# Attention of one layer on one core: the values product two tiles behind the scores, projections in the spare halves of the score banks, three queues written in a new order, and the causal bias matmul moved from first to third place in its group

## The reference

```
q_latent, kv_latent = xn @ wq_down, xn @ wkv_down            # 192 and 64 wide
q = concat(q_latent @ wq_nope, rope(q_latent @ wq_rope))     # per head 128 + 64
k = concat(kv_latent @ wk_nope, rope(kv_latent @ wk_rope))
scores = where(causal, q k^T / sqrt(192), min);  probs = softmax(scores)
out = (probs @ (kv_latent @ wv_up)).reshape(b, t, 16 * 192) @ wo
x = x + out + mixture_of_experts(xn)                          # top 8 of 32 experts
```

## Time and profile before

| | us |
|---|---|
| median of 3 runs (lowest, highest) | 1311.97 (1310.3, 1316.01) |
| the profiled execution's own time | 1314.4 |
| its span, first to last instruction | 1312.6 |
| PE busy in the span | 1161.8 (89%) |
| DVE, ACT, POOL busy | 720.3 (55%), 646.2 (49%), 493.9 (38%) |
| attention, from its first score matmul to the first matmul of the experts | 69.3 to 901.7 |

### The profile page before, as it was taken

One profiled execution on the slowest core, in us unless ns is written; L12 is line 12 of the kernel. 1 busy time (PEld: TensorE's weight loads), 2 busy tenths in 40 slices (PEclk: granted clock), 3 DMA queues, 4 the chain that ended last, 5 costly groups with the idle time before them and its releaser, 6 DMA issues. The chain is left out here.

```text
span 1312.6 us, 23292 instructions
## 1 busy us (share of the span) xinstructions
PE 1161.8 (89%) x7616; PEld 936.2 (71%) x7616; DVE 720.3 (55%) x1298; ACT 646.2 (49%) x1287; POOL 493.9 (38%) x386
## 2 busy tenths in 40 slices
PE   6678889888888898898888988998999999999997
PEld 3456667667677676676776766776788887888886
DVE  6556756556555556565555565554444445444444
ACT  3545556555555565555555555664433333333332
POOL 1263534543444445335444453421333332333332
PEclk9989999999999999999999999998999999999999
DMA  5001001000000000100000000103633333533332
GB/s 194 33 0 32 1 1 32 1 0 26 5 0 2 28 0 0 31 0 0 31 0 0 15 0 1 57 25 97 198 112 115 112 114 107 143 114 111 113 112 88
DMA packets 26304, 67.35 MB, mean 51 GB/s; under 512 B 3029, under 2 KB 9557, under 8 KB 26265
## 3 DMA queue, kind: packets, MB, share of 16 engines
q1 hardware_dynamic: 26120, 66.78, 16.6%
q10 hardware_dynamic: 144, 0.07, 0.0%
HBM read 62.36 MB, written 4.47 MB: 51 GB/s over the span
## 5 line engine op out<-in xcount | busy, mean ns | idle before, releaser
L714 ACT ACTIVATE prob<-ps_s,nm 128x128 f32<-128x128 f32 (+7 forms) x256 | 189.5, 740 | 203.3 <-DVE nm L866 200.9
L1305 POOL TENSOR_TENSOR hl<-hf,hh 128x512 fp32r<-128x512 f32 x96 | 123.5, 1286 | 294.9 <-ACT hh L1242 294.9
L866 DVE TENSOR_REDUCE nm<-ps_s 128x1 f32<-128x128 f32 (+7 forms) x256 | 192.3, 751 | 70.5 <-PE ps_s L548 69.0
L571 PE MATMUL ps_o<-pt,kvn 128*64 128x128 f32 x2304 | 154.0, 277 | 64.5 <-DVE pt L875 49.5
L571 PEld LDWEIGHTS ps_o<-pt,kvn 128*64 128x64 f32 x2304 | 126.2, 136 | 100.9 <-ACT pt L724 51.2
L559 PE MATMUL ps_t<-ident,prob 128*128 128x128 f32 x1152 | 173.0, 276 | 9.4 <-DVE pt L875 6.7
L1017 POOL TENSOR_TENSOR xtf<-xtf,sinv 128x512 f32<-128x512 f32 x62 | 79.4, 1280 | 223.4 <-DVE xtf L835 221.2
L559 PEld LDWEIGHTS ps_t<-ident,prob 128*128 128x128 f32 x1152 | 138.7, 142 | 32.2 <-issue 10.9
L1032 POOL TENSOR_TENSOR qlo<-t,qhi 64x512 fp32r<-64x512 f32 x64 | 82.0, 1281 | 159.8 <-ACT qhi L751 147.2
L724 ACT ACTIVATE pt<-ps_t 128x128 f32<-128x128 f32 (+2 forms) x192 | 96.6, 503 | 88.1 <-PE ps_t L559 86.7
L875 DVE COPY pt<-ps_t 128x128 f32<-128x128 f32 (+2 forms) x192 | 101.6, 529 | 56.2 <-PE ps_t L559 55.3
(11 more groups left out here) (272 smaller groups left out, 2689.5 us busy)
## 6 DMA issues: line engine op xcount, KB each, us to landing
routing<-wT_scratch SPq DMA_DIRECT2D x34, 256.0 KB, 3.7
raw_a<-in_e SPq DMA_DIRECT2D x17, 384.0 KB, 3.1
cosv<-in_e SPq DMA_DIRECT2D x17, 384.0 KB, 3.1
sinv<-wT_scratch SPq DMA_DIRECT2D x17, 384.0 KB, 3.6
raw<-in_e SPq DMA_DIRECT2D x17, 384.0 KB, 3.0
routing<-wT_scratch SPq DMA_DIRECT2D x16, 384.0 KB, 3.3
raw_a<-in_a SPq DMA_DIRECT2D x8, 512.0 KB, 3.3
raw_b<-in_b SPq DMA_DIRECT2D x8, 480.0 KB, 3.9
```

Source lines behind the costliest of these rows:

```text
L571: mm = nc.tensor.matmul(ps_o[64 * e:64 * e + 64, at], kvn[:, b * 8 + j, :], pt[t % 2][:, e, j, :], start=j == 0, stop=j == t)
L714: nc.scalar.activation(prob[t % 2][e][:, 0:len(halves) * width].rearrange("p (h k) -> p h k", k=width), ps_s[e][:, 0:len(halves), 0:width] ...
L866: nc.vector.tensor_reduce(out=nm[:, e:e + 1], in_=ps_s[e][:, 0:len(halves), 0:halves[0][1]], axis=AXXY, op=ALU.max, negate=True).then_inc( ...
L1305: nc.gpsimd.tensor_tensor(hl[:, c, :], hf[:, c, :], hh[:, c, :].bitcast(F32), ALU.subtract).then_inc(h_lo, 1)
```

## The change

The values product of step `t` is now that of tile `t - 2` (`before_tile(..., lag=2)`), and it stands between the turns of head 0 and those of head 1 of tile `t - 1`, not at the end of the step. Six kinds of side work (`Lp`, `QR1`, `KR0`, `KR1`, and `W1`, `W3` of the last stage) no longer use `ps_x`: up to tile 3 the second bank of `ps_s[0]` or `ps_s[1]` lies idle, and they take it (`SPARE`, `bank_of`); the scores of tile 4 wait until it has been read. `STAGE` and the three queues of PE, ACT and DVE are written in a new order, and POOL takes the low part of the first `QR` after all four sums. The causal bias matmul stands between the second and the third fp32r pass. `split_a` reads PSUM first, so that the bank is free two operations earlier. No matmul, transpose, copy or transfer is added or taken away.

```
-STAGE = ["Lp", "QR0", "KR0", "QL0", "QR1", "L0", "Yp0", "KR1", "QL1", "Yp1", "B", "WA", "Y0", "Y1"]
+STAGE = ["QR0", "Lp", "KR0", "QL0", "QR1", "KR1", "Yp0", "Yp1", "L0", "B", "QL1", "WA", "Y0", "Y1"]
+SPARE = {"Lp": 0, "QR1": 0, "W3": 0, "KR0": 1, "KR1": 1, "W1": 1}
...
+    if spare is not None:
+        earlier = [x for x in order[:order.index((b, name))] if x[0] == b and SPARE.get(x[1]) == spare]
+        return (i, *earlier[-1]) if earlier else None
...
+            return ps_s[SPARE[name]][:, 1, :] if name in SPARE else ps_x
...
-        def before_tile(i, b, t):
+        def before_tile(i, b, t, lag=1):
             s = i * 2 + b
-            return (s, b, t - 1) if t else (s - 1, 1 - b, TILES - 1)
+            return (s, b, t - lag) if t >= lag else (s - 1, 1 - b, TILES + t - lag)
...
             if name == "WA":
-                return a_split, (0 if b is None else i + 1) * 4 + 4
+                return a_split, (0 if b is None else i + 1) * 4 + 2
...
+                if t == TPC and half == 1:
+                    held = ("KR1" if e else "QR1") if not is_last(i, b) else "W1" if e else "W3"
+                    pe.wait_ge(*consumed(i, b, held))
...
+                nc.tensor.matmul(out[:, 0:width], qhi[b][e][:, q], khi[b][e][:, kk], start=True, stop=False, skip_group_check=True)
+                nc.tensor.matmul(out[:, 0:width], qhi[b][e][:, q], klo[b][e][:, kk], start=False, stop=False, skip_group_check=True)
                 if diagonal:
-                    nc.tensor.matmul(out[:, width - P:width], mask16[:, :], ident16[:, :], start=True, stop=False, skip_group_check=True)
-                nc.tensor.matmul(out[:, 0:width], qhi[b][e][:, q], khi[b][e][:, kk], start=not diagonal, stop=False, skip_group_check=True)
-                nc.tensor.matmul(out[:, 0:width], qhi[b][e][:, q], klo[b][e][:, kk], start=False, stop=False, skip_group_check=True)
+                    nc.tensor.matmul(out[:, width - P:width], mask16[:, :], ident16[:, :], start=False, stop=False, skip_group_check=True)
                 mm = nc.tensor.matmul(out[:, 0:width], qlo[b][e][:, q], khi[b][e][:, kk], start=False, stop=True, skip_group_check=True)
...
+                        def products():
+                            if earlier or t > 1:
+                                values(*before_tile(i, b, t, 2))
...
                         elif t < TPC:
                             scores(i, b, t, 0, 0)
-                            turn(sp, tp, 0, 0)
-                            turn(sp, tp, 1, 0)
+                            turns(0)
+                            also("QL0" if t == 2 else "QR1")
+                            products()
+                            turns(1)
                             scores(i, b, t, 1, 0)
-                            values(sp, bp, tp)
-                            also(("KR0", "QL0", "QR1")[t - 1])
+                            if t == 3:
+                                also("KR1")
...
-                            also(("KR1", "Yp1", "WA")[t - TPC - 1])
-                            scores(i, b, t, 1, 0)
-                            turn(sp, tp, 1, 0)
-                            turn(sp, tp, 1, 1)
-                            scores(i, b, t, 1, 1)
+                            if t < TILES - 1:
+                                also(("L0", "QL1")[t - TPC - 1])
+                            products()
                             if t == TILES - 1:
                                 also("Y0")
-                            values(sp, bp, tp)
-                            also(("QL1", "B", "Y1")[t - TPC - 1])
+                            scores(i, b, t, 1, 0)
+                            turns(1)
+                            scores(i, b, t, 1, 1)
+                            also(("B", "WA", "Y1")[t - TPC - 1])
...
-                        rope_low(s + 1, 0, 1 - b, (rope_sum, s * 4 + 7))
-                        rope_low(s + 1, 1, 1 - b, (rope_sum, s * 4 + 7))
                         rope_sum_of(s + 1, 3)
+                        rope_low(s + 1, 0, 1 - b, (rope_sum, s * 4 + 8))
```

More of the change, by code:

```diff
@@ L660, in body @@
                             scores(i, b, t, 0, 0)
-                            turn(sp, tp, 0, 0)
                             scores(i, b, t, 0, 1)
-                            also("L0")
-                            turn(sp, tp, 1, 0)
+                            turns(0)
+                            also("Yp0")
+                            products()
+                            turns(1)
                             scores(i, b, t, 1, 0)
                             scores(i, b, t, 1, 1)
-                            values(sp, bp, tp)
@@ L668, in body @@
-                            also("Yp0")
+                            also("Yp1")
                         else:
@@ L688, in _ @@
             s, t = 2 * PAIRS - 1, TILES - 1
-            for e in range(2):
-                for g in range(2):
-                    turn(s, t, e, g)
+            for g in range(2):
+                turn(s, t, 0, g)
+            values(s, 1, t - 1)
+            for g in range(2):
+                turn(s, t, 1, g)
             pe.wait_ge(widened, s * 2 + 2)
@@ L912, in body @@
                         has = earlier or t > 0
+                        if more and t == 1:
+                            rope_products(i, b, "QR0", s + 1)
+                        if more and t == 2:
+                            rope_products(i, b, "KR0", s + 1)
+                        if more and t == 3:
+                            latent_low(i, b, 0, s + 1, 1 - b)
+                        if more and t == TPC:
+                            rope_products(i, b, "KR1", s + 1)
+                        if t == TPC + 1 and earlier:
+                            add_out(misc(i, b, "Yp1"), ps_x, s - 1, 1 - b, 1, 1)
@@ L913, in body @@
+                        if t == TPC + 2 and b == 0:
+                            split_b(i, b)
+                        if t == TPC + 3 and b == 0 and not is_last(i):
+                            split_a(i, b, i + 1)
+                        maximum(s, t, 0)
+                        if has and (t == 0 or t > TPC):
+                            take_turned(sp, tp, 0, 1)
                         if t == 0 and earlier:
                             invert(s - 1, 1)
+                        if more and t == 3:
+                            rope_products(i, b, "QR1", s + 1)
@@ L929, in body @@
-                        if more and t == TPC + 1:
-                            rope_products(i, b, "KR1", s + 1)
-                        if t == TPC + 2 and earlier:
-                            add_out(misc(i, b, "Yp1"), ps_x, s - 1, 1 - b, 1, 1)
-                        if t == TPC + 3 and b == 0 and not is_last(i):
-                            split_a(i, b, i + 1)
-                        if has and t > TPC:
-                            take_turned(sp, tp, 1, 1)
-                        maximum(s, t, 1)
@@ L938, in body @@
-                        if has and t == 0:
-                            take_turned(sp, tp, 1, 1)
-                        if t == 0 and earlier:
-                            normalise(s - 1, 1)
-                        if more and t in (0, 1, 3):
-                            rope_products(i, b, ("QR0", "KR0", None, "QR1")[t], s + 1)
-                        if more and t == 2:
-                            latent_low(i, b, 0, s + 1, 1 - b)
-                        if t == TPC:
-                            normalise(s, 0)
-                            if earlier:
-                                add_out(misc(i, b, "Yp0"), ps_x, s - 1, 1 - b, 1, 0)
@@ L952, in body @@
+                        if t == 1 and earlier:
+                            normalise(s - 1, 1)
                         if t == TILES - 1:
-                            for m in range(2):
-                                add_out(misc(i, b, f"Y{m}"), ps_x, s, b, 0, m)
+                            add_out(misc(i, b, "Y1"), ps_x, s, b, 0, 1)
                         if is_first(i) and b == 0 and t in (5, 6, 7):
```

160 lines of the change are left out of this document (90 added, 70 removed).

## The result

The changed kernel takes 1206.32 us (median of 4 runs, 1205.4 to 1207.15), the kernel before 1311.13 in the same sitting: a ratio of 0.9194, 95% interval 0.9169 to 0.922. That is 104.8 us less, where 85 were forecast.

The account below looks back on a forecast made before the run. PE's stream sets the pace and loses time by waiting, 112.5 us idle in the attention. 1314.4 - 108 removed + 23 back = 1229.4, predicted 1229 us; range leaving out two in ten 1204 to 1280.

Parts of the forecast that it names:

- the 112.5: Attention: PE's idle time of 112.5 us, taken as the most that an order of the same work can give back.
- The waits: PE's waits in the attention: 103.0 us of five kinds and half of 9.5 small ones go, 108 us removed.
- 23 back: Costs set against the 108 us removed: `WA` 6, tile 3 4, bias 3, first pair and last stage 4, missed waits 6.
- `WA`: PE's wait at the weights' fold behind `QL1`, b = 0 only: about 0.8 us in 7 pairs, 6 us back.
- Tile 3's start: Tile 2 to tile 3: DVE and ACT need 3.7 us, PE about 3.4; 0.3 late per stage, 4 us back.
- the 0.4 in each stage: Allowance in every attention stage for waits that a count misses: 6 us back.
- the same 89 to 90 us of PE work: Sign of being right: a steady pair takes about 92 us (before 103.60) with PE's work unchanged.
- The bias: Causal bias matmul in third place, 256 groups: 0.12 us for all, 3 us lost; bounds 20 us gained, 26 lost.
- the values' 61: Values product's waits for its copies (49.5 + 11.6 us): 61.1 us go with values two tiles behind.
- The spreading's 23.5: Spreading of the reciprocals waits for ACT's widening: 23.5 us go because widening, `Lp` and `L0` stand later.
- the table's 11.7: Output projection's wait for readers of `ps_x`, behind `QL1`'s low parts: 11.7 us go with spare banks and new table.
- slower, by DVE's queue: Rival: 1.74 us of wait at each of five DVE places in 15 stages, 130 us, giving 1337 us; chance 0.06.

## Why the prediction was right, and where its sum was off

The direction held. The range held by luck: 1206 lies 2 us above its lower end of 1204, and with the pairs written out the same change takes 1193, below it. The sum is compared with that version, which has no disturbed edges; its attention is 832.42 - 712.10 = 120.3 us shorter. That is more than the 112.5 which I called the most that an order of the same work can give back: I had taken PE's own work as fixed.

*The waits.* Right in kind, and larger than forecast; a steady pair takes 88.48 us, where about 92 were forecast: idle time fell by 112.5 - (712.10 - 700.56) = 101 us, where 108 - 20 = 88 were forecast (23 back, less the bias's 3). `WA` came back with 2.3 us in the changed kernel, not 6. Tile 3's start (4) and the 0.4 in each stage for waits that a count by hand misses (6) were nothing: a steady pair has 0.54 us of idle time in all, 0.4 of it at `WA`.

*PE's own work: the term that was mis-sized.* I wrote that a steady pair would keep "the same 89 to 90 us of PE work" and added 3 for the bias. It fell from 89.57 to 87.94, in the attention by 719.95 - 700.56 = 19.4 us. Some 15 of these are the pairs, 8 x 1.85 (89.68 to 87.83); most of the rest is the clock, since three pairs of the kernel before ran in part at its lower level (a mean granted clock of 0.95 in the first, 0.98 at 484 and at 588). For the pairs, the run with one bank shows the mechanism: the run-out behind a wait is counted as work, 0.23 to 0.24 us where turns stand ahead of a projection. Before, 19 waits of over 0.15 us stood in one pair, now one. With the bias in first place in both, 18 waits fewer went with 89.57 - 87.37 = 2.2 us less work, about 0.12 each; how this divides over the kinds of wait, and over waits too short to be listed, was not measured. The place of the values product is no part of it.

*The bias.* 0.12 us for all groups, 3 us: measured 3.0 by the pairs of the changed kernel. In the kernel before the times say 2.9, but the pairs less than 0.1 each. The rule of the Trainium skill ("TensorE: Matmul & The Clock Gate", Part 2) that weight loads are pulled ahead, by which some 20 us would have been gained, did not show its gain in either kernel.

*Which edit does what.* I priced each edit by its own row of waits, and this step failed, though the sum did not show it. The lag alone is worth 82.8 us and takes the values' 61. The spreading's 23.5, which I put to the reciprocals' later place, went without it, but 13.3 of them by way of a new wait at `Y1`; what the later place is worth where `Y0` and `Y1` stand apart was not tried by itself. The spare banks, to which I put the table's 11.7, are worth 5.0 us a pair, 40 in eight, but only in the new order, and against waits which that order makes (`QL0` for `KR0`'s reader, `QR1` for `QL0`'s). In one bank the new order, 93.48 us a pair, is no better than the lag alone in the old one, 92.64; together, with the bias first in both, order and banks are worth 92.64 - 88.11 = 4.5 us a pair. Without the lag the rest is 29 us slower than before, with 30.9 of wait for the normalisation and 95.5 for copies at the values line. My rival "slower, by DVE's queue" is what that run looks like, though DVE's order was not tried by itself. Two tiles of lag are what made it harmless: with the values product last in the step in both, one tile takes 1341 us and two take 1210.

*What I had not named.* The disturbed edges, some 14 us against the gain. They brought the time toward my forecast: with the pairs written out it is 1193 us, 36 under 1229.

## What to carry to other kernels

Take a wait's price from the distance of two starts with and without it, not from the wait's row: the run-out of the last matmul belongs to it. Edits of order can't be summed from rows of before: moving the values product out from between two uses of a shared bank made a wait of 19.9 us that no row of before had. For each piece that moves, look at what it stood between, and price the lag, the order and the banks together. Once an engine is busy for 95% of the span, look at the edges of its loops; here writing out the iterations took the ratio from 0.9194 to 0.9097.

## What the runs showed of the hardware

The jump back of a loop can cost PE about 7 us: 4.0 to 4.3 us of standing still and a stretch at the lower clock. It came at two of the edges in the changed kernel's profile and at none in the profile with the bias first, and by the times of that kernel its number differs from run to run. Each time the trace holds nine more instruction packets of 16 KB (41 against 23). On the clock of the timeline the first of them start at 330.17 and 514.33 us, 2.2 and 2.1 us before PE stands still; in the runs with one bank and with the values last, five more disturbed edges have the first packet 1.0 to 2.4 us ahead of the stop. The windows around the stop at 332.37 show two packets (14 GB/s x 2.37 us, 33 KB) and then none:

```profile
330.00:332.37 2.37, 2.37 (x15) 1.57 (x13) 1.42 (x3) 1.81 (x4) 1.06 (x1) 1.00 0.08 14
332.37:335.07 2.70, 0.00 (x1) 0.01 (x1) 1.16 (x2) 1.21 (x2) 1.50 (x2) 1.00 0.00 0
```

The order in time, and the run with the pairs written out, fit a fetch of the loop's body that PE waits for. That PE waits for these packets is still not shown, since the trace does not say whose instructions they hold, and what decides at which edge it comes stays open. In straight code the packets come one by one all through the attention (52 in all) and PE does not wait for them.
